# Per-sample LoRA factors summed on VectorE inside the stages, instead of in a stage of their own ahead of them

## The reference

```
q = layernorm(x)                                   # over the 2048 channels
corr = ifft(fft(q) * conj(fft(ctx))).real          # over the 512 rows, per channel
w, lag = top_k(corr, 12); w = softmax(w)
x = x + sum_i w_i * ctx[min(lag_i + row, 511)]     # attention by autocorrelation

h = layernorm(x)
A_eff[b] = sum_n gate[b, n] * lora_A[n]            # 16 adapters, rank 32
B_eff[b] = sum_n gate[b, n] * lora_B[n]
x = x + h @ W + bias + B_eff[b] (A_eff[b] h) + B_shared (A_shared h)
```

## Time and profile before

| | |
|---|---|
| median of 3 timed runs | 3331.47 us (3331.15 to 3333.57) |
| profiled execution, whole | 3328.88 us |
| its span, first to last instruction | 3327.1 us |
| TensorE busy | 3171.9 us, 95% |
| VectorE busy | 1884.1 us, 57% |
| GpSimd busy | 1672.9 us, 50% |
| ScalarE busy | 1132.1 us, 34% |
| mean granted TensorE clock | 0.979 of 2.4 GHz |

### The profile page before, as it was taken

One profiled execution on the slowest core, in us unless ns is written; L12 is line 12 of the kernel. 1 busy time (PEld: TensorE's weight loads), 2 busy tenths in 40 slices (PEclk: granted clock), 3 DMA queues, 4 the chain that ended last, 5 costly groups with the idle time before them and its releaser, 6 DMA issues. The chain is left out here.

```text
span 3327.1 us, 39244 instructions
## 1 busy us (share of the span) xinstructions
PE 3171.9 (95%) x15104; PEld 1742.4 (52%) x15104; DVE 1884.1 (57%) x2621; ACT 1132.1 (34%) x1784; POOL 1672.9 (50%) x760
## 2 busy tenths in 40 slices
PE   7499999999989999999976999999999999999999
PEld 5355665665655665665633444444444444444444
DVE  4288988888878999999972232321323232132322
ACT  1456666666656666555511110110111011011100
POOL 0578988988878988988752211221122122112210
PEclk9799999999999999999987999999999999999999
DMA  7223344234334454344228111111011111101110
GB/s 311 98 105 133 118 146 157 105 135 158 118 139 143 146 171 165 114 131 158 76 83 284 61 64 61 39 61 64 34 53 64 61 39 61 64 26 60 64 51 26
DMA packets 126450, 344.58 MB, mean 104 GB/s; under 512 B 7744, under 2 KB 24256, under 8 KB 108864
## 3 DMA queue, kind: packets, MB, share of 16 engines
q1 hardware_dynamic: 126272, 341.96, 29.3%
HBM read 253.59 MB, written 88.34 MB: 103 GB/s over the span
## 5 line engine op out<-in xcount | busy, mean ns | idle before, releaser
L1336 PE MATMUL ps<-w_hi,h_hi 128*128 128x512 f16 x2048 | 780.5, 381 | 17.7 <-issue 17.7
L1337 PE MATMUL ps<-w_lo,h_hi 128*128 128x512 f16 x2048 | 780.1, 381 | 0.0
L1338 PE MATMUL ps<-w_hi,h_lo 128*128 128x512 f16 x2048 | 779.2, 380 | 0.0
L1229 POOL TENSOR_TENSOR xt<-xt,vl 128x2048 f32<-128x2048 f32 x32 | 144.1, 4504 | 1013.5 <-DMA xt<-x_scratch 750.2
L917 PE MATMUL ps<-op,it 128*128 128x512 f32 x1024 | 447.4, 595 | 12.8 <-DVE op L1026 12.8
L1443 DVE SCALAR_TENSOR_TENSOR xt<-ps,w_back,xt 128x512 f32<-128x512 f32 x128 | 96.0, 750 | 625.0 <-PE ps L1338 623.9
L849 PE MATMUL ps<-wt,fp 128*128 128x512 f16 x1536 | 338.3, 380 | 1.4 <-DVE wt L993 1.4
L1336 PEld LDWEIGHTS ps<-w_hi,h_hi 128*128 128x128 f16 x2048 | 201.1, 98 | 257.2 <-issue 29.9
L1338 PEld LDWEIGHTS ps<-w_hi,h_lo 128*128 128x128 f16 x2048 | 201.2, 98 | 244.2 <-issue 4.4
L917 PEld LDWEIGHTS ps<-op,it 128*128 128x128 f32 x1024 | 195.2, 191 | 247.4 <-issue 230.6
L1337 PEld LDWEIGHTS ps<-w_lo,h_hi 128*128 128x128 f16 x2048 | 201.1, 98 | 229.1 <-issue 3.2
(11 more groups left out here) (167 smaller groups left out, 5735.5 us busy)
## 6 DMA issues: line engine op xcount, KB each, us to landing
cg<-ctx SPq DMA_DIRECT2D x32, 1024.0 KB, 5.1
xg<-x SPq DMA_DIRECT2D x32, 1024.0 KB, 8.4
xv<-x SPq DMA_DIRECT2D x32, 1024.0 KB, 5.1
x_scratch<-xv SPq DMA_DIRECT2D x32, 1024.0 KB, 5.2
xt<-x_scratch SPq DMA_DIRECT2D x32, 1024.0 KB, 5.0
out<-xt SPq DMA_DIRECT2D x32, 1024.0 KB, 3.9
xrow<-x SPq DMA_DIRECT2D x24, 1024.0 KB, 5.1
xrow<-w SPq DMA_DIRECT2D x16, 1024.0 KB, 5.0
```

The lines of the kernel that those rows point to most:

```text
L1229: nc.gpsimd.tensor_tensor(xt[:, k, :], xt[:, k, :], vl[:, :], ALU.add).then_inc(vl_ok, 1)
L1336: nc.tensor.matmul(ps[:, c, :], h_hi[:, k, i, :], w_hi[:, i, cols], start=(i == 0), stop=False)
L1337: nc.tensor.matmul(ps[:, c, :], h_hi[:, k, i, :], w_lo[:, i, cols], start=False, stop=False)
L1338: last = nc.tensor.matmul(ps[:, c, :], h_lo[:, k, i, :], w_hi[:, i, cols], start=False, stop=(i == KT - 1))
```

## The change

The adapter stage is gone, and its parts stand elsewhere.

- **Start of attention.** SP loads the Fourier table, the first context group and the rows of sample 0 at once, then the rows of sample 1, into tiles that attention uses later (`x_first`, `x_second`). VectorE takes the statistics of both samples (`first_statistics`) ahead of the first correlation products, and GpSimd makes the scale and shift of sample 0 (`first_rows`) between its first operations. The prologue's order on ScalarE changes: `normalise(0, 2)` and `high_of_u(0, 2)` stand behind the exponentials.
- **Sums of sample 0.** The host lays each adapter out as one 128 x 1024 tile (A and B together). In each of the steps 0 to 15 SP loads one adapter into `wc` (idle until step 16) with its gate, and VectorE adds it to a running sum that lies where the Fourier table was, ahead of `products_even`. The sum goes to DRAM before step 16.
- **Largest weight.** `partition_all_reduce` is replaced by a transpose and a 1-row matmul on TensorE, inside the transposes of step 16.
- **Sums of samples 1 to 7.** In each of the tiles 0 to 2 of a sample the output stage loads six adapters (four in tile 2) and VectorE adds them for the next sample, three behind `rest_of_h` and three behind `finish` 2. The B part goes through DRAM once per sample.
- **Scales.** They are taken per sample, from the sum over partitions of the row maxima (one matmul with a matrix of ones, `bounds`), with some small VectorE operations (`read_bound`, `scales`) ahead of `high_of_ab`.

Three sums stand ahead of each of the last two finishes. The diff, cut to its core:

```diff
-        with ExitStack() as st:                      # the whole adapter stage, L161 to L329
...
@@ attention, SP
+                    def load_adapter(b, g):
+                        n = GPB * b + g
+                        if later(b, g):
+                            sp.wait_ge(gate_ok, n)
+                        sp.dma_start(wc[:, :], lora_ab[n]).then_inc(s_gate, 16)
+                        sp.dma_start(gsc[:, :], gate[0, bass.ds(n, 1)].partition_broadcast(P)).then_inc(s_gate, 16)
...
+                    sp.dma_start(ft[:, :, :, :], fwd_tab).then_inc(s_ft, 16)
+                    load_v_row(sp, 0, 0)
+                    load_ctx(sp, 0, 0)
+                    for t in range(TT):
+                        sp.dma_start(x_first[t], x_g[0, :, t, :]).then_inc(s_xs[0][t], 16)
+                    sp.dma_start(fp[:, :, :, :, :], fwd_pair).then_inc(s_tabs, 16)
+                    sp.dma_start(nyq[:, :], nyq_mask).then_inc(s_tabs, 16)
+                    load_row(0, 1)
+                    load_ctx(sp, 0, 1)
+                    sp.dma_start(it[:, :, :], inv_tab).then_inc(s_tabs, 16)
+                    sp.dma_start(ident[:, :], eye).then_inc(s_tabs, 16)
+                    for t in range(TT):
+                        sp.dma_start(x_second[t], x_g[1, :, t, :]).then_inc(s_xs[1][t], 16)
...
@@ attention, GpSimd
                     subtract_row(0, 0)
+                    rest_of_u(0, 0)
+                    subtract_row(0, 1)
+                    first_rows(0)
                     fold_q(0, 0)
-                    rest_of_u(0, 0)
                     rest_of_q(0, 0)
-                    subtract_row(0, 1)
                     fold_q(0, 1)
                     rest_of_u(0, 1)
                     corr_sums(0, 0)
+                    first_rows(1)
                     rest_of_q(0, 1)
...
-                    pool.wait_ge(top_ok, 1)
-                    nc.gpsimd.partition_all_reduce(wtop[:, 1:2], wtop[:, 0:1], P, bass.bass_isa.ReduceOp.max).then_inc(topall_ok, 1)
@@ attention, TensorE, transpose_w
+                        if scale:
+                            pe.wait_ge(top_ok, 1)
+                            nc.tensor.transpose(ps[0:1, 3, 0:P], wtop[:, 0:1], ident[:, :]).then_inc(top_spec, 1)
                         for k in range(4):
+                            if scale and k == 3:
+                                pe.wait_ge(row_max, 1)
+                                nc.tensor.matmul(ps[:, 3, P:P + 1], ones[0:1, :], wtop[0:1, 1:2], start=True, stop=True).then_inc(topall_ok, 1)
+                                pe.wait_ge(top_read, 1)
@@ attention, VectorE
+                            dve.wait_ge(gate_ok, n)
+                            nc.vector.scalar_tensor_tensor(out=ab_sum, in0=wc[:, :], scalar=gsc[:, 0:1], in1=ab_sum,
+                                                           op0=ALU.mult, op1=ALU.add).then_inc(gate_ok, 1)
...
                         if convert:
                             weights_rest(b, g, 0)
+                        else:
+                            add_adapter(b, g)
                         products_even(b, g)
...
+                    first_statistics(0)
+                    first_statistics(1)
                     corr_products(0, 0)
@@ output stage, SP
+                        for i in range(6 * t, min(6 * t + 6, NL)):
+                            if later(b, t) or i > 1:
+                                sp.wait_ge(g_ok, NL * b + i - 1)
+                            sp.dma_start(sg[:, i % 2, :, :].rearrange("p s c -> p (s c)"), lora_ab[i]).then_inc(s_sg[i % 2], 16)
+                        if t == TT - 2:
+                            sp.wait_ge(g_ok, NL * b + NL)
+                            sp.wait_ge(ab_lo, 16 * b + 16)
+                            sp.dma_start(b_next, ab[:, 2, :]).then_inc(s_bst, 16)
+                            sp.wait_ge(s_bst, 16 * b + 16)
+                            load_b(b + 1, b_next)
@@ output stage, TensorE
+                    def bounds(b, bank, col):
+                        pe.wait_ge(mx_ok, b + 1)
+                        nc.tensor.matmul(ps[:, bank, col:col + 4], ones[:, :], mx[:, :], start=True, stop=True).then_inc(sc_spec, 1)
@@ output stage, VectorE, step and start
                         if more:
                             rest_of_h(*nxt)
+                        if gated and t < TT - 1:
+                            gated_part(b, t, 0)
                         finish(b, t, 2)
+                        if gated and t < TT - 1:
+                            gated_part(b, t, 1)
+                            if t == TT - 2:
+                                dve.wait_ge(g_ok, NL * b + NL)
+                                largest(b + 1)
                         finish(b, t, 3)
...
+                    nc.vector.tensor_reduce(mx[:, 1:2], ab[:, 1, :], AXX, ALU.max, apply_absolute_value=True)
+                    nc.vector.tensor_reduce(mx[RANK:2 * RANK, 3:4], b_f[RANK:2 * RANK, :], AXX, ALU.max, apply_absolute_value=True)
+                    largest(0)
+                    read_bound(0)
+                    scales(0)
                     rest_of_ab(0)
```

More of the change, by code:

```diff
@@ L50 @@
 HSCALE = 1024.0
-AXSCALE = 2.0 ** -21
+AXSCALE = 2.0 ** -17
 ER, EI, OR, OI = range(4)
@@ L943, in _ @@
                         step(0, g, True, True)
-                    with pe.Fori(1, B - 1) as b:
+                    pe.wait_ge(eps_ok, 2)
+                    with pe.Fori(1, B // 2) as b:
+                        for g in range(GPB):
+                            step(b, g, True, True)
+                    for g in range(GPB):
+                        step(B // 2, g, True, True, g == 0)
+                    with pe.Fori(B // 2 + 1, B - 1) as b:
                         for g in range(GPB):
@@ L1141, in build @@
             s_ab = sem("s_ab", st)
+            s_sg = [sem(f"s_sg{k}", st) for k in range(2)]
+            s_gt = sem("s_gt", st)
+            s_bst = sem("s_bst", st)
+            g_ok = sem("g_ok", st)
+            mx_ok = sem("mx_ok", st)
+            sc_spec = sem("sc_spec", st)
+            sc_read = sem("sc_read", st)
+            sc_ok = sem("sc_ok", st)
+            own3 = sem("own3", st)
+            s_first = sem("s_first", st)
             ab_hi = sem("ab_hi", st)
@@ new lines, in gated_part, with largest, read_bound @@
+                    def gated_part(b, t, part):
+                        first = 6 * t + 3 * part
+                        for i in range(first, min(first + 3, NL)):
+                            gated_sum(b, i)
+                    def largest(b):
+                        nc.vector.tensor_reduce(mx[:, 0::2], ab[:, 0::2, :], AXX, ALU.max, apply_absolute_value=True).then_inc(mx_ok, 1)
+                    def read_bound(b):
+                        col, bank = (2 * P, 5) if later(b, 0) else (0, 0)
+                        dve.wait_ge(sc_spec, b + 1)
+                        nc.vector.tensor_reduce(bound[:, :], ps[:, bank, col:col + 4].rearrange("p (a s) -> p a s", s=2), AXX, ALU.add).then_inc(sc_read, 1)
@@ L1447, in step @@
+                    def step(b, t, more, gated):
                         n, nxt = TT * b + t, ahead(b, t, 1)
                         rest_of_ax(b, t)
+                        if gated and t == TT - 1:
+                            read_bound(b + 1)
                         if more:
@@ L1453, in step @@
                         add_adapter(b, t)
-                        if more and t == TT - 1:
+                        if gated and t == TT - 1:
+                            scales(b + 1)
                             rest_of_ab(b + 1)
```

409 lines of the change are left out of this document (185 added, 224 removed).

## The result

The changed kernel takes 3308.88 us in the median of 5 runs (3307.43 to 3316.2), the kernel before 3331.15 us on the same chip (5 runs, 3327.37 to 3333.57). The ratio is 0.9939, with a 95% interval of 0.9925 to 0.9954: faster by 22 us. The forecast was 73 us faster, 3258 us, with a range that ended at 3286. The direction was right, the size was not.

What follows compares the result with a forecast made beforehand. The prediction took TensorE to bound the steady attention steps and the output stage, but not the adapter stage, pipeline filling or half way. Terms -86 - 5 + 5 + 8.5 + 4 = -73.5 us gave 3258 us, range 3238 to 3286.

Steps and rivals of the forecast that it cites:

- Start, -86: Start of attention: step 0's transposes begin at 85.7 us instead of 171.7, 86 us less; ends 76 and 105.
- Sums in the steady step, +5: Steady attention steps: even products 2.8 us late, about 0.35 us left in each of 15 steps, 5 us more.
- 2.45 us of cover: Steady attention step: weights ready at 660.08 us, taken by TensorE at 662.53, so 2.45 us of delay would be hidden.
- Landing of the data, 7.0 us: Steady attention step: the adapter's load takes 7.0 us to land, so the sum runs from 627.5 to 628.8.
- Its upper end, 32 us: Steady attention steps: each sum takes 3.08 us instead of 1.27 beside working GpSimd, 32 us over 15 steps.
- The query's load 2 us later, so nothing.: Steady attention steps: two added issues delay the query's 1 MB load about 2 us; ScalarE catches up, no cost.
- A: Theory of the experiments, not the prediction: late sum data, passed on by the correlation's wait for even products, cost 60 us.
- Half way, -5: Four steps half way: GpSimd's standstill goes, ScalarE is late next; 5 us less, between nothing and 17.8.
- Seam, +8.5: Seam to output stage: 6 us waiting for scales, 2.5 us for tile 0's fourth finish; 8.5 us more, 4 to 16.
- Output stage and TensorE's additions, +4: Output-stage sums hide and cost nothing; TensorE's small matmul, weight loads and code sections cost 4 us more, 0 to 10.
- Rival 2: Steady attention steps: sums push VectorE past its cover, 32 instead of 5 us, 3285 us in all; chance 19%.

Runs made afterwards that it cites:

- e5: e1 with three more operations of the sum's kind and size on VectorE ahead of the sum: 3372.32 us.
- e5b: e1 with one more operation of the sum's size on VectorE ahead of the sum: 3269.97 us.
- e1: Changed kernel with each steady step's adapter and gate loads issued one step ahead, the sum at its place: 3244.72 us.
- e3: Changed kernel with only the first 8 of 1024 columns summed from the second adapter on, loads and waits kept: 3295.93 us.
- e2: Changed kernel with all 16 gates of the first sample loaded once at the start, no gate load per step: 3295.91 us.
- e4: Changed kernel with the steady step's sum moved behind the odd products, loads still late: 3266.94 us.
- e6: e4 with the adapter and its gate issued behind the query's load in the same step: 3257.41 us.
- e8: e1 with the half-way maximum of the weights taken again by GpSimd's reduction over all partitions: 3254.52 us.
- e7: Changed kernel with the adapter and gate issued behind the query's load, the sum still ahead of the even products: 3371.97 us.

## Why the prediction was wrong

- **Start, -86.** Right: -83.6. The chain through `turn_row` was 3 us longer than worked out. GpSimd had the second context group at 24.3 us, where 21 was taken.
- **Sums in the steady step, +5.** This step failed, with +60.0. Wrong was the sentence "2.45 us of cover". I went down VectorE's chain to its last result, the weights, and compared only this with the moment TensorE wants it. But TensorE also waits for an intermediate link, the even products, to overwrite their PSUM banks, and there the cover was 0.49 us. With the forecast's own delay of 2.8 us this alone makes 2.3 us in 15 steps, 35 us by estimate. The data were also later than forecast, 5.0 us behind VectorE's last product in the mean (4.3 forecast), which makes the delay 3.5 us in the mean instead of 2.8: another 10. The rest was not in the sum at all: every step with a wait lost 0.3 us beside it, and idle TensorE comes back at a lower clock in seven of 15 steps, 16 us together. e5 and e5b measured the cover, e1 took the lateness away, e3 kept it without the work.
- **Landing of the data, 7.0 us.** That 4.3 us came near the 4.27 us of the step shown is luck. The prediction gave 7.0 us to the adapter, which landed in 5.3 to 6.2. It gave nothing to the gate's small load, which was issued behind it and was the last to land in all 15 steps.
- **Its upper end, 32 us.** The prediction put it down to VectorE and GpSimd in each other's way, 3.08 us instead of 1.27. In the changed kernel the sums paid little of this. Nine took 1.28 us, since they came when GpSimd was through, and six took 1.5 to 2.1, 0.18 us more in the mean of the 15. The rule of the Trainium skill (page "SBUF — State Buffer", section "Who interferes with whom"), that the two exclude each other for a whole instruction and the second one blocks, agrees with the rows: e5 shows 3.29 and 3.36 us and e5b 3.39, with GpSimd's 2.37 become 3.27 beside them, and e2's 3.25 us ended 1.1 us behind GpSimd's operation. In e1 the sum starts just ahead of GpSimd's first addition and takes 1.28, and this addition takes 3.34.
- **"The query's load 2 us later, so nothing."** Half right. In the changed kernel A's delay covers it; e4 against e6 shows 9.5 us for it once A is gone.
- **Half way, -5.** Right: -6.0 in the traces; the reduction by itself is worth 7.7 in e8.
- **Seam, +8.5.** Right, and by its parts: +8.4, of which 5.2 were forecast as 6 and 3.3 as 2.5.
- **Output stage and TensorE's additions, +4.** That the sums hide was right. The +4 for TensorE's own additions, for which the prediction named no row, did not come: +0.7 and -0.9. No run measured them alone, and the dips of the clock in five tiles move this stretch by more.
- **Rivals.** Rival 2 came nearest, an overrun of the cover in steady steps, but by another mechanism and with 32 us for what cost 60. No rival had TensorE waiting for the even products, and the range, ended at rival 2's price, missed the time by 23 us.

## What to carry to other kernels

Before an instruction is put into the idle time of an in-order engine, list every wait of other engines on anything that the engine makes behind it, buffer releases included, and take the smallest cover on the list, not the last. Give the new operation's data a whole step's lead: moving two DMA issues, the adapter's and its gate's, was worth 64 us here, with the arithmetic unchanged. And price an idle microsecond of a saturated TensorE at more than one: in the mean of 15 steps 1.0 us cost 1.3, 2.9 us cost 4.0 and 5.8 us cost 8.4 us per step.

## What the runs showed of the hardware that I had not expected

- A load of 0.5 KB, 4 bytes to each of 128 partitions, landed 5.6 to 7.0 us after its issue (6.7 in the median). It stood behind 1.5 MB on the same queue; the 0.5 MB adapter just ahead of it took 5.3 to 6.2 us. In e7, with the query's 1 MB ahead of both, it took 8.6 us in the median, in e1 5.6.
- Two VectorE operations of the same form, side by side with GpSimd, took 3.3 us each instead of 1.28, and slowed GpSimd's from 2.37 to 3.27 us. In e5 the two engines' operations end in turn: GpSimd's at 610.6 us, VectorE's at 611.6, GpSimd's at 613.8, VectorE's at 614.9. The same operation just ahead of GpSimd's took 1.28, so order by a fraction of a microsecond decides 2 us.
- TensorE's granted clock over the 6 us behind an idle time: 1.00 after 1.0 to 1.1 us in all 15 steps of e5b; in the changed kernel 1.00 after 2.4 to 3.1 us in eight steps and 0.72 to 0.76 after 2.3 to 4.5 us in seven; 0.50 to 0.76 after 4.9 to 7.4 us in every step of e5 and e7. e2 has steps at 1.00 after up to 3.3 us and at 0.72 and 0.73 from 2.3 us on. So between 2.3 and 3.3 us it went either way in the attention steps, and in the output stage up to 3.5 us; no run here shows what decides it.
